# Weight pieces split ahead of the step loop, and GpSimd's elementwise instructions cut into parts: a fused macaron attention layer on one core

## What is computed

```
x = x + 0.5 * FFN(layernorm(x))
x = x + Attention(layernorm(x))
x = x + 0.5 * FFN(layernorm(x))
```

```
q = rope((x @ Wq)); k = rope((x @ Wk)); v = x @ Wv
scores = einsum('bgrtd,bgsd->bgrts', q, k) * D ** -0.5     (causal)
out = softmax(scores) @ v;   return out.reshape(B, T, H * D) @ Wo + bo
```

## Time and profile before

| | us |
|---|---|
| median of 3 runs (lowest, highest) | 1462.56 (1459.61, 1463.27) |
| the profiled execution's own time | 1462.43 |
| its span in the profile | 1460.6 |
| busy: PE, DVE, ACT, POOL | 1384.1, 1180.8, 961.5, 721.1 |
| mean granted TensorE clock | 0.978 |

### The profile page before, as it was taken

How to read it: one execution, slowest core, us unless ns; L and a number is a source line. 1 busy time by engine, 2 the same in 40 slices (tenths; PEclk the granted TensorE clock), 3 DMA queues, 4 the chain that set the end, 5 groups by cost and what they waited for, 6 DMA issues and landing times.

```text
span 1460.6 us, 26285 instructions
## 1 busy us (share of the span) xinstructions
PE 1384.1 (95%) x8818; PEld 779.6 (53%) x8818; DVE 1180.8 (81%) x2816; ACT 961.5 (66%) x2423; POOL 721.1 (49%) x603
## 2 busy tenths in 40 slices
PE   5678999998999999999999999999999999999995
PEld 4335555554555655555555555555555555555543
DVE  6788968889988888889778788889777798868655
ACT  3467777676776766676766776666666777666733
POOL 0278766667765454435545354444543454344312
PEclk9699999999999999999999999999999999999997
DMA  7168766777767566656557566557565667464433
GB/s 234 44 165 205 192 158 175 191 178 196 176 144 173 135 126 134 138 119 153 129 128 167 127 134 145 119 131 141 139 138 136 135 146 161 120 141 103 98 76 116
DMA packets 439398, 210.54 MB, mean 144 GB/s; under 512 B 382016, under 2 KB 383232, under 8 KB 439264
## 3 DMA queue, kind: packets, MB, share of 16 engines
q1 hardware_dynamic: 437152, 204.66, 60.5%
q10 hardware_dynamic: 2112, 4.19, 0.9%
HBM read 90.30 MB, written 25.17 MB: 79 GB/s over the span
## 4 chain that ended last, share of the span: by engine, by line
PE 77%; DVE 11%; ACT 4%; issue 4%; POOL 3%; DMA 1%; DVEq 0%; SPq 0%; ACTq 0%
PE PJ L1191 17%; PE PJ L1193 17%; PE PJ L1192 17%; PE PV L1191 4%; PE PV L1193 4%; PE PV L1192 4%; PE SC L1357 4%; PE SC L1356 4%; PE SC L1355 4%; DVE phl L1008 3%; POOL t L530 2%; ACT p L685 2%; DVE p L998 2%; DVE t L971 1%; DVE t L969 1%
## 5 line engine op out<-in xcount | busy, mean ns | idle before, releaser
L538 POOL TENSOR_TENSOR oTl<-of,oTf 128x512 f16<-128x512 f32 x128 | 154.2, 1204 | 444.3 <-ACT oTf L677 444.2
L685 ACT ACTIVATE p<-p,mn 128x512 f32<-128x512 f32 (+3 forms) x512 | 280.8, 549 | 98.4 <-DVE mn L998 98.3
L1008 DVE SCALAR_TENSOR_TENSOR phl<-p,ri,phl 128x128 f16<-128x128 f32 (+3 forms) x512 | 333.2, 691 | 0.0
L1191 PE MATMUL PJ<-XT,wsp 128*128 128x512 f16 x640 | 244.4, 382 | 4.8 <-DVE t L971 1.7
L696 ACT ACTIVATE phl<-p,ri 128x128 f16<-128x128 f32 (+3 forms) x512 | 245.6, 550 | 4.1
L1192 PE MATMUL PJ<-XT,wsp 128*128 128x512 f16 x640 | 244.2, 382 | 0.0
L1193 PE MATMUL PJ<-XT,wsp 128*128 128x512 f16 x640 | 244.0, 381 | 0.0
L530 POOL TENSOR_TENSOR t<-t 128x512 f32<-128x512 f32 x160 | 204.7, 1279 | 72.8 <-DVE t L971 72.5
L998 DVE CUSTOM_DVE_ANT_0 p<-SC,maskw 128x512 f32<-128x512 f32 (+3 forms) x512 | 219.8, 485 | 2.1
L533 POOL TENSOR_TENSOR qTl<-t,qTh 128x512 f16<-128x512 f32 x128 | 148.4, 1159 | 93.2 <-ACT qTh L664 93.2
L1192 PE MATMUL PJ<-wosp,oTf 128*128 128x512 f16 x512 | 194.1, 379 | 0.0
(11 more groups left out here) (204 smaller groups left out, 2644.9 us busy)
## 6 DMA issues: line engine op xcount, KB each, us to landing
wsp<-kept SPq DMA_DIRECT2D x144, 256.0 KB, 3.0
wosp<-kept SPq DMA_DIRECT2D x96, 256.0 KB, 3.4
raw<-in_wqkv SPq DMA_DIRECT2D x48, 256.0 KB, 4.7
kept<-wsp SPq DMA_DIRECT2D x48, 256.0 KB, 2.4
raw<-in_wo SPq DMA_DIRECT2D x32, 256.0 KB, 4.7
kept<-wosp SPq DMA_DIRECT2D x32, 256.0 KB, 3.0
X<-in_x ACTq DMA_DIRECT2D x4, 1024.0 KB, 10.9
pTf<-phl SPq DMA_TRANSPOSE x256, 3.8
```

Source lines behind the costliest of these rows:

```text
L538: nc.gpsimd.tensor_tensor(oTl[:, n % 2, h, :], of[:, s % 2, :], oTh[:, n % 2, h, :], ALU.subtract).then_inc(o_lo, 1)
L685: ins = nc.scalar.activation(pt, pt, ACT.Exp, bias=mn[:, par, i:i + 1], scale=-1.0, accum_out=rs[:, par, i:i + 1])
L1008: nc.vector.scalar_tensor_tensor(out=phl[:, par, low(i, 0):low(i, i) + 1, :], in0=p[:, par, SOFF[i]:SOFF[i] + w].rearrange("p (k t) -> p k ...
L1191: mm(out_, lh, rh, start=start, stop=False)
```

## The change

It does two things. Twenty pieces, all of units 0 and 1, are split ahead of the steps instead of seven. Those of unit 1 that go to `wsp`, whose slots unit 0 still holds, are split in idle buffers (`oTl` and `of`), stored in DRAM, and loaded from there in steps 0 to 2 (STAGED); TensorE waits for that load instead of for `weight_low`. Each raw slot is filled again right behind the `keep` of the piece that freed it. And GpSimd's instructions are cut in parts along the free dimension: two parts each, four for the weights, one for the penalty as before. `made` lists the pieces still split in the steps: none in steps 0 and 1, K(2) in step 2, and W pieces only from step 10.

```diff
-HEAD_ITEMS = [(0, "K"), (0, "Q0"), (0, "V"), (0, "Q1"), (0, "Q2"), (0, "Q3"), (1, "K")]
+HEAD_ITEMS = ([(0, k) for k in ("K", "Q0", "V", "Q1", "Q2", "Q3", "W0", "W1", "W2", "W3")]
+              + [(1, k) for k in KINDS])
+
+STAGED = [(1, k) for k in PIECES]
-    out = [(1, "Q0")] if s == 0 else []
+    out = [(1, "K"), (1, "Q0")] if s == 0 else []
...
+def made(s):
+
+    return [it for it in refills(s) if it[0] < G and it not in HEAD_ITEMS]
...
+        def made_slot(kind, n):
+            if (n, kind) not in STAGED:
+                return weight_slot(kind, n)
+            k = PIECES.index(kind)
+            if k < 4:
+                return oTl[:, k // 2, 2 * (k % 2):2 * (k % 2) + 2, :]
+            return of[:, k - 4, :].bitcast(F16).rearrange("p (m n) -> p m n", m=2)
+
+        def loads_before(kind, n):
+
+            e = 1 if kind in PIECES else 0
+            return 0 if n == 1 else n - G + e
...
                 if n < G + 2:
-                    sp.wait_ge(st_w[kind], 16 * G)
-                if n > G:
-                    sp.wait_ge(ld_s[kind], 16 * (n - G))
+                    sp.wait_ge(st_w[kind], 32 if n == 1 else 16 * G)
+                if loads_before(kind, n):
+                    sp.wait_ge(ld_s[kind], 16 * loads_before(kind, n))
                 sp.dma_start(weight_slot(kind, n), kept_at(kind, n)).then_inc(ld_s[kind], 16)
...
-            for r in range(6):
+            for r in range(NHEAD):
                 keep(r)
+                raw_load(r + NRAW)
             for s in range(NS):
                 for n, kind in refills(s):
-                    if n >= G:
+                    if n >= G or (n, kind) in STAGED:
                         load_kept(n, kind)
-                for r in range(6, len(ITEMS)):
+                for r in range(NHEAD, len(ITEMS)):
...
+            def parts(k):
+
+                return [slice(i * T // k, (i + 1) * T // k) for i in range(k)]
...
-                nc.gpsimd.tensor_tensor(X[:, n, :], X[:, n, :], bob[:, :], ALU.add).then_inc(bo_add, 1)
+                for c in parts(2):
+                    ins = nc.gpsimd.tensor_tensor(X[:, n, c], X[:, n, c], bob[:, c], ALU.add)
+                ins.then_inc(bo_add, 1)
...
-                nc.gpsimd.tensor_tensor(both[:, C:2 * C], normal_of(k, bb, i), both[:, 0:C],
-                                        ALU.subtract).then_inc(ln_lo[k], 1)
+                hi, lo, x_ = both[:, 0:C], both[:, C:2 * C], normal_of(k, bb, i)
+                for c in parts(2):
+                    ins = nc.gpsimd.tensor_tensor(lo[:, c], x_[:, c], hi[:, c], ALU.subtract)
+                ins.then_inc(ln_lo[k], 1)
...
-                nc.gpsimd.tensor_tensor(w[:, 1, :], raw[:, r % NRAW, :], w[:, 0, :].bitcast(BF16),
-                                        ALU.subtract).then_inc(w_lo, 1)
+                for c in parts(4):
+                    ins = nc.gpsimd.tensor_tensor(w[:, 1, c], raw[:, r % NRAW, c], w[:, 0, c].bitcast(BF16), ALU.subtract)
+                ins.then_inc(w_lo, 1)
...
-                nc.gpsimd.tensor_tensor(t1[:, j, :], t1[:, j, :], t2[:, j, :], ALU.add).then_inc(rope_sum, 1)
+                for c in parts(2):
+                    ins = nc.gpsimd.tensor_tensor(t1[:, j, c], t1[:, j, c], t2[:, j, c], ALU.add)
+                ins.then_inc(rope_sum, 1)
...
-                nc.gpsimd.tensor_tensor(lo, t1[:, j, :], hi, ALU.subtract).then_inc(rope_lo, 1)
+                for c in parts(2):
+                    ins = nc.gpsimd.tensor_tensor(lo[:, c], t1[:, j, c], hi[:, c], ALU.subtract)
+                ins.then_inc(rope_lo, 1)
...
-                nc.gpsimd.tensor_tensor(oTl[:, n % 2, h, :], of[:, s % 2, :], oTh[:, n % 2, h, :],
-                                        ALU.subtract).then_inc(o_lo, 1)
-
+                if s == 0:
+                    for kind in PIECES[:4]:
+                        pool.wait_ge(st_w[kind], 32)
+                for c in parts(2):
+                    ins = nc.gpsimd.tensor_tensor(oTl[:, n % 2, h, c], of[:, s % 2, c], oTh[:, n % 2, h, c], ALU.subtract)
+                ins.then_inc(o_lo, 1)
+
+            for r in range(6):
+                weight_low(r)
             penalty(0, 0)
-            for r in range(6):
+            for r in range(6, NHEAD):
                 weight_low(r)
             for kind, n, idx, _ in FIRST:
                 if kind in "QK":
                     rope(kind, n, idx)
-            weight_low(6)
...
-                    if it[0] < G:
-                        weight_low(ITEM[it])
+                for it in made(s):
+                    weight_low(ITEM[it])
...
-                if n >= (2 if kind[0] == "W" else 1):
+                if n >= 2:
                     act.wait_ge(*weight_used(kind, n))
-                    act.wait_ge(st_w[kind], 16 * (n - 1 if kind[0] == "W" else n))
-                nc.scalar.copy(weight_slot(kind, n)[:, 0, :].bitcast(BF16), raw[:, r % NRAW, :]).then_inc(w_hi, 1)
+                    act.wait_ge(st_w[kind], 16 * n)
+                nc.scalar.copy(made_slot(kind, n)[:, 0, :].bitcast(BF16), raw[:, r % NRAW, :]).then_inc(w_hi, 1)
...
+                if s == 0:
+                    for kind in PIECES[4:]:
+                        act.wait_ge(st_w[kind], 32)
...
+            for r in range(NRAW):
+                weight_high(r)
             act.wait_ge(fs_pe, 8)
             nc.scalar.copy(v2h[:, :], PV[:, :]).then_inc(fs_hi, 1)
             act.wait_ge(ld_fs, 96)
             gelu(0, 0)
             exps_ffn(0, 0)
             gate_exp(0, 0, 4)
-            weight_high(0)
+            weight_high(8)
+            weight_high(9)
             e_hi(0, 0)
             logs(0)
             gate_exp(1, 0, 4)
             for i in range(4):
                 base(0, 0, i)
-            weight_high(1)
-            weight_high(2)
+            for r in range(10, 16):
+                weight_high(r)
             root(0, 1, 4, NT)
+            weight_high(16)
+            weight_high(17)
             root(1, 0, 0, 4)
-            weight_high(3)
+            weight_high(18)
+            weight_high(19)
             for i in range(4):
                 turned_hi(1, 0, i)
             act.wait_ge(cst0, 1)
             nc.scalar.activation(warm[:, :], ones[:, 0:1], ACT.Exp)
-            weight_high(4)
-            weight_high(5)
...
+                if n < G and (n, kind) not in STAGED:
                     pe.wait_ge(w_lo, ITEM[(n, kind)] + 1)
                 else:
-                    pe.wait_ge(ld_s[kind], 16 * (n - G + 1))
+                    pe.wait_ge(ld_s[kind], 16 * (loads_before(kind, n) + 1))
```

More of the change, by code:

```diff
@@ L152 @@
 for s_ in range(NS):
-    for it_ in refills(s_):
-        if it_[0] < G:
-            ITEMS.append(it_)
-            MADE_AT.append(s_)
+    for it_ in made(s_):
+        ITEMS.append(it_)
+        MADE_AT.append(s_)
 ITEM = {it: r for r, it in enumerate(ITEMS)}
+NHEAD = len(HEAD_ITEMS)
 def macaron_kernel(nc: bass.Bass, x, wqkv, wo, bo, cosq, sinq, cosk, sink,
@@ L422, in keep @@
                 sp.wait_ge(w_lo, r + 1)
-                sp.dma_start(kept_at(kind, n), weight_slot(kind, n)).then_inc(st_w[kind], 16)
+                sp.dma_start(kept_at(kind, n), made_slot(kind, n)).then_inc(st_w[kind], 16)
             def load_kept(n, kind):
@@ L465, in _ @@
                 raw_load(r)
-            for r in range(6):
+            for r in range(NHEAD):
                 keep(r)
+                raw_load(r + NRAW)
             for s in range(NS):
                 for n, kind in refills(s):
-                    if n >= G:
+                    if n >= G or (n, kind) in STAGED:
                         load_kept(n, kind)
-                for r in range(6, len(ITEMS)):
+                for r in range(NHEAD, len(ITEMS)):
                     if MADE_AT[r] + 2 == s:
                         keep(r)
-                for r in range(NRAW, len(ITEMS)):
-                    if max(MADE_AT[r - NRAW] + 2, 0) == s:
+                for r in range(NHEAD + NRAW, len(ITEMS)):
+                    if MADE_AT[r - NRAW] + 2 == s:
                         raw_load(r)
@@ L515, in normal_lo @@
                 pool.wait_ge(ln_hi[k], 4 * bb + i + 1)
-                nc.gpsimd.tensor_tensor(both[:, C:2 * C], normal_of(k, bb, i), both[:, 0:C],
-                                        ALU.subtract).then_inc(ln_lo[k], 1)
+                hi, lo, x_ = both[:, 0:C], both[:, C:2 * C], normal_of(k, bb, i)
+                for c in parts(2):
+                    ins = nc.gpsimd.tensor_tensor(lo[:, c], x_[:, c], hi[:, c], ALU.subtract)
+                ins.then_inc(ln_lo[k], 1)
             def weight_low(r):
                 n, kind = ITEMS[r]
-                w = weight_slot(kind, n)
+                w = made_slot(kind, n)
                 pool.wait_ge(w_hi, r + 1)
-                nc.gpsimd.tensor_tensor(w[:, 1, :], raw[:, r % NRAW, :], w[:, 0, :].bitcast(BF16),
-                                        ALU.subtract).then_inc(w_lo, 1)
+                for c in parts(4):
```

(14 more changed lines are left out.)

1 line of the change is left out of this document (removed).

## The result

The change takes 1457.3 us (median of 9 runs, 1456.33 to 1458.47) beside 1461.7 for the kernel before: a ratio of 0.9975, 95% interval 0.9965 to 0.9985. That is 4.4 us faster where 22 were forecast, and outside the range of 1431 to 1454. The span of the profiled execution falls from 1460.6 to 1456.1 us.

A forecast was written before the change was run, and what follows sets the result against it. TensorE was taken to wait for VectorE, itself held by GpSimd's instructions, in start and middle; the head is a dependent chain. 1462.4 + 1.2 (head) - 8.5 (start) - 15 (middle) = 1440 us, range 1431 to 1454.

The forecast's parts named there:

- VectorE is held by GpSimd's current instruction: Start and middle: each VectorE instruction waits for what is left of one GpSimd instruction, so shorter ones shrink its waits.
- 0.35 / 4 + 0.65 / 2: Middle: share of VectorE's waits left, 0.41, with weights (35% of GpSimd's time) in quarters and the others halved.
- From VectorE's relief to TensorE's time: Middle: VectorE relieved by 16.5 us, TensorE's waits in `attend` nearly vanish; 15 of 13.0 + 5.7 us won.
- What the parts cost GpSimd: Middle: 0.03 us fixed per added part, from memsets; 5.6 us in all, GpSimd at 137 us.
- What GpSimd's time is worth: Middle: GpSimd's busy time, 137 us or 168 at 0.20 us per part, set against 170 us available.
- the rival of costly parts: GpSimd, 0.15 to 0.2 us fixed per part: middle gives 4, start 6, head costs 2; 1454 us, chance 0.12.
- The middle's 15 us: Steps 13 to 29: 15 us won from TensorE's idle time and clock; ends 5 and 18.
- The start's 8.5 us: Steps 0 to 5: 8.5 us won, mostly from 10.3 us of VectorE's waits removed, clock's recovery included.
- my ends of 4 and 14: Start: the low and high end of the gain taken as 8.5 us.
- The head's +1.2 us: Before the first scores: ScalarE's added weights cost 0.7 us, VectorE's small operations beside GpSimd 0.5; ends 0 and 4.
- Later steps at nothing: From step 30 on: every step as long as before, nothing won or lost.

The follow-up runs named there:

- e16: The change with, in the steps, weights whole and all other GpSimd instructions in halves (head in parts as in the change): 1460.0 us.
- e15: The change with, in the steps, weights in quarters and all other GpSimd instructions whole (head as in the change): 1447.1 us.
- e1: The change without parts, every GpSimd instruction whole: 1458.2 us.
- e14: The change with parts only ahead of step 0, there halves instead of quarters, and whole instructions in all steps: 1456.7 us.
- e12: The change with, in the steps, weights in halves and all other GpSimd instructions whole (head as in the change): 1450.1 us.
- e20: The change with, in the steps, weights in eighths and all other GpSimd instructions whole (head as in the change): 1469.7 us.
- e13: The change with the weights made in the steps in eight parts instead of four, all other parts kept: 1484.8 us.
- e18: The change with its rotary sums in one instruction each, all else in parts as it has it: 1454.0 us.
- e9: The change with only the first 8 columns of each weight's low half made in a step computed, other parts kept: 1441.5 us.
- e11: The change with only 8 columns of each weight's low half made in a step, whole instructions in the steps, parts in the head: 1439.2 us.
- e6: The change with parts only ahead of step 0 (weights in quarters there) and whole GpSimd instructions in every step: 1456.6 us.
- e2: The kernel before with all the change's parts and nothing else of it, seven pieces split ahead of the steps: 1470.9 us.
- e3: The change with weights in two parts instead of four: 1456.3 us.
- e5: The change with as many GpSimd instructions, but the added ones of a single column, so that one long instruction stays: 1461.8 us.
- e7: The change with whole GpSimd instructions in the head and steps 0 to 25, parts from step 26 on: 1462.2 us.
- e17: The change with every GpSimd instruction in the steps in halves, weights included (head as in the change): 1457.2 us.

## Why the prediction was wrong

- **VectorE is held by GpSimd's current instruction: right.** L1008 in the middle was forecast at 46 us and took 47.2; VectorE's busy time at 151, and it was 149.5. L844 there takes 0.73 us (forecast 0.9). But that the 46 came out is in part luck. I had spread the waits over all instructions by their time or number, "0.35 / 4 + 0.65 / 2", so that the halved others gave more than half of the relief of L1008. By e16 they give it next to nothing, and the weights' quarters alone (e15) give most of it.
- **From VectorE's relief to TensorE's time: it did not pass.** With VectorE relieved by 16.5 us I took 15 of TensorE's 18.7 us of idle time and clock as won. The relief came, but TensorE's waits for turned probabilities stayed (11.3 and 10.6 us), since the exponentials now waited for GpSimd's sums. The next term is why.
- **What the parts cost GpSimd: the step that failed.** I took 0.03 us per part from the memsets, 5.6 us in the middle. Measured are 32. In the row of the head's first six weights a weight takes 9.30 / 6 = 1.55 us in quarters, for 1.12 whole (6.73 / 6, e1) and 1.27 in halves (7.59 / 6, e14), 0.14 per added instruction:

```profile
24.12 9.30 POOL L554 TENSOR_TENSOR wsp<-raw,wsp 128x128 f16<-128x128 f32 x24 [21.80 <-ACT wsp L697]
```

  The sum of the rotary embedding, 1.279 us in the earlier trace rows, takes 232.8 / 160 = 1.455 in two, 0.18 more:

```profile
L562 POOL TENSOR_TENSOR t<-t 128x256 f32<-128x256 f32 x320 | 232.8, 749 | 43.0 <-DVE t L1014 42.4
```

  And in the middle, beside VectorE, 46.67 / 39 = 1.20 us per weight become 1.43 in halves (e12), 1.87 in quarters (e15), 2.49 in eighths (e20): 0.23, 0.22 and 0.18 per added instruction. Some 185 of them made 131.49 us into 163.7, not 137. The memset was the wrong row: an instruction that reads two inputs has a larger fixed part than the interval between two memsets shows. The Trainium skill (GPSIMD Engine Reference, Elementwise: side-by-side cycle accounting) gives about 2.6 cycles per element for two inputs, and from this and the row of 1.279 us came an estimated 31 us for the 185. The trace agrees: the rise is 32. I had named that case and given it 0.12, where it should have been the forecast.
- **What GpSimd's time is worth: a second error, in the same comparison.** I set its busy time against 170 us. But 15.3 us of the middle pass between a rotary sum and ScalarE's cast of it, and can't be filled. Even the rival of costly parts, which had 160 to 168 of 170, came out at 1454 by leaving the middle a gain of 4; it had none. That the cost is what took the gain is shown from both sides: more parts on the weights lengthen the middle (e13, e20), fewer parts on the others bring gain back (e15, e18).
- **The middle's 15 us: there, but not to be had by parts.** With GpSimd's work on weights away the middle wins 16.1 and 17.5 us (e9, e11), so the stage can give that much. The change won nothing: relief and cost cancel. 5.6 to 6.4 us can be had with the weights' parts alone (e12, e15). What parts without cost would win, no run shows.
- **The start's 8.5 us:** 5.6 up to step 5 and no more up to step 12, within my ends of 4 and 14. But the cause is not the one that I gave most of it to. With whole instructions the start wins 5.6 and 7.2 us up to step 12 (e1, e6): it comes with the weights moved ahead of the steps (nine fewer here), and the parts give nothing there; where the fourteen stay, the parts lose 8.9 (e2). The clock is 0.92 there, where above 0.93 was forecast.
- **The head's +1.2 us:** the second root starts at 53.34 (forecast 53.1), the first scores at 73.99 (forecast 75.2, before 73.97), the last ten weights end at 64.5 instead of 61, still 2 us ahead of the first rotary sum. The first exponential is 0.6 us sooner than before, which the scatter of this head covers. Two raw loads did come late, and ScalarE waited 0.65 and 1.37 us for them, but it had its last weight done before `turned_hi` could start. By the traces the parts are needed here: +3.8 us with whole weights (e1). In the medians of e1 and e6 that is 1.6 us, which is not resolved.
- **Later steps at nothing: open in its size.** The nine kernels with both sums and low halves in parts there (the change, e2, e3, e5, e7, e9, e13, e16, e17) lose 1.3 to 4.7 us behind step 29. Kernels with equal, whole steps lose 0 to 1.7, and e11, whole but with the largest lead, 2.4. The change loses 1.6 of its 1.8 up to step 38 and nothing from step 48 on.

## What to carry to other kernels

Cutting one engine's instructions to relieve another engine is a trade: count the added instructions, price each with a two-input instruction of that engine (here 0.14 to 0.23 us on GpSimd), and set the sum against the waits for work that is not there yet, not against all idle time. Cut those that stand beside the held instructions (here the weights), leave whole those in the chain that other engines wait for (here the rotary sums), and stop while the engine still has some slack. And busy time taken off an engine is no time won: the anchor is the operation that the next stage waits for, which here was the exponential and not the minimum ahead of it.

## What the hardware showed that I had not expected

- An added two-input instruction of GpSimd, the columns in all staying the same, costs 0.14 us in the rows of the head (1.12, 1.27 and 1.55 us per weight in one, two and four parts). In the middle, where VectorE takes turns with it, it costs 0.23 for the cut in two, 0.22 each up to quarters ((1.87 - 1.43) / 2) and 0.16 each up to eighths ((2.49 - 1.87) / 4).
- VectorE's operations of 4 columns (0.16 us each in the kernel before, while GpSimd is idle) take 1.08 us each beside a queue of 512-column instructions of GpSimd (e1), and 0.35 beside quarters (the change). In this chain of three, each paid nearly a whole weight of GpSimd, 1.12 us.
- Single columns cut off long instructions shorten VectorE's low halves as much as true quarters do (0.70 in e5 against 0.66 us each), at about the same cost (GpSimd busy for 164.9 and 163.7 us in the middle). What the turns' rule is in detail, these runs don't tell.
